# One kernel, three edits: a third home for the normalised rows of the first stage, the key-value product in four strips, and a gate by tanh in place of the sigmoid

## The reference

```python
xn = _layernorm(x, axis=-1)
x = x + _L0_attn_ref(xn, Wq, Wk, Wv) + _L0_ffn_ref(xn, Wr, br, W1, b1, W2, b2)
xn = _layernorm(x, axis=-1)
x = x + _L1_attn_ref(xn, W_qkv, W_out) + _L1_ffn_ref(xn, W_r, W_k, W_v, mu_r, mu_k)

# _L1_attn_ref, after rotation of q and k by position:
q_feat = jax.nn.elu(q * SCALE) + 1.0
k_feat = jax.nn.elu(k) + 1.0
kv = jnp.einsum('bhtd,bhtv->bhdv', k_feat, v)        # per head 16 x 16
k_sum = k_feat.sum(axis=2)
denom = jnp.maximum(jnp.einsum('bhtd,bhd->bht', q_feat, k_sum), 1e-06)
out = jnp.einsum('bhtd,bhdv->bhtv', q_feat, kv) / denom[..., None]

# _L1_ffn_ref:
r = jax.nn.sigmoid(jnp.einsum('btc,dc->btd', xr, W_r))
k = jnp.einsum('btc,dc->btd', xk, W_k)
out = r * jnp.einsum('btc,dc->btd', jnp.square(jax.nn.relu(k)), W_v)
```

## Time and profile before

| what | value |
|---|---|
| median of 3 runs | 980.91 us (980.83 to 981.66) |
| the profiled execution | 979.83 us, its span 978.2 us |
| TensorE busy | 865.8 us, 89% of the span |
| VectorE busy | 674.3 us, 69% |
| ScalarE busy | 515.4 us, 53% |
| GpSimd busy | 181.2 us, 19% |
| mean granted TensorE clock | 0.955 |

### The profile page before, as it was taken

The page is one execution under the profiler, slowest core; times in us unless marked ns, Lnnn a source line. Parts: engine busy times, 40 slices in busy tenths (PEclk is TensorE's granted clock), DMA queues, the critical chain, the costliest instruction groups (busy, mean ns, idle before and its releaser), DMA issues. The chain is left out here.

```text
span 978.2 us, 16165 instructions
## 1 busy us (share of the span) xinstructions
PE 865.8 (89%) x5619; PEld 773.9 (79%) x5619; DVE 674.3 (69%) x1287; ACT 515.4 (53%) x907; POOL 181.2 (19%) x198
## 2 busy tenths in 40 slices
PE   3898202799799999999999999999979999999998
PEld 3687101799699999899999989999878787978877
DVE  7786000454666878878787787888477979889764
ACT  3632000433555564664756465475438867678581
POOL 1004775000000000000000000000612526153202
PEclk9999555899999999999999999999989999999999
DMA  8772446000544766666567665653300203021101
GB/s 263 265 253 76 151 156 218 1 1 2 163 131 150 230 229 214 214 220 209 190 207 244 216 211 203 221 197 103 92 23 22 65 19 98 16 76 53 43 1 44
DMA packets 93871, 134.24 MB, mean 137 GB/s; under 512 B 8608, under 2 KB 78688, under 8 KB 93824
## 3 DMA queue, kind: packets, MB, share of 16 engines
q1 hardware_dynamic: 85024, 107.80, 33.6%
q0 software_dynamic: 8800, 25.83, 7.9%
HBM read 98.22 MB, written 35.39 MB: 137 GB/s over the span
## 5 line engine op out<-in xcount | busy, mean ns | idle before, releaser
L1061 PE MATMUL ps<-w2h,hh 128*128 128x256 f32 x568 | 162.8, 287 | 0.0
L1063 PE MATMUL ps<-w2h,hl 128*128 128x256 f32 x568 | 160.7, 283 | 0.0
L1062 PE MATMUL ps<-w2l,hh 128*128 128x256 f32 x568 | 160.7, 283 | 0.0
L1201 ACT ACTIVATE h<-ps,b1T 128x512 f32<-128x512 f32 (+1 forms) x160 | 90.5, 588 | 132.7 <-PE ps L1063 132.5
L1306 DVE TENSOR_TENSOR hl<-h,hh 128x512 fp32r<-128x512 f32 x124 | 85.5, 689 | 66.1 <-ACT hh L1205 65.2
L1061 PE MATMUL ps<-xTh,w1h 128*128 128x512 f32 (+1 forms) x320 | 110.7, 346 | 2.4 <-DVE xTl L1248 2.4
L1050 POOL DMA_DIRECT2D expert_out<-y x28 | 20.5, 733 | 492.3 <-DVE y L1265 492.3
L1062 PE MATMUL ps<-xTl,w1h 128*128 128x512 f32 (+1 forms) x320 | 110.6, 346 | 0.0
L1061 PEld LDWEIGHTS ps<-w2h,hh 128*128 128x128 f32 x568 | 108.7, 191 | 2.4 <-DVE hl L1306 0.2
L1062 PEld LDWEIGHTS ps<-w2l,hh 128*128 128x128 f32 x568 | 108.8, 192 | 2.1
L1063 PE MATMUL ps<-xTh,w1l 128*128 128x512 f32 (+1 forms) x320 | 109.9, 343 | 0.0
(11 more groups left out here) (306 smaller groups left out, 2262.9 us busy)
## 6 DMA issues: line engine op xcount, KB each, us to landing
raw<-in_L_ffn_W SPq DMA_DIRECT2D x30, 1024.0 KB
raw_odd<-in_L_ffn_W SPq DMA_DIRECT2D x28, 1024.0 KB, 6.8
dispatched<-shared SPq DMA_DIRECT2D x1, 9088.0 KB, 32.1
expert_out<-y POOLq DMA_DIRECT2D x11, 512.0 KB, 3.6
rows<-dispatched SPq DMA_DIRECT2D x20, 256.0 KB, 3.4
shared<-in_L_ffn_b SPq DMA_DIRECT2D x9, 512.0 KB, 8.3
xn_rows<-raw SPq DMA_DIRECT2D x4, 1024.0 KB, 5.2
rows<-xn_rows SPq DMA_DIRECT2D x32, 128.0 KB
```

Source lines behind the costliest of these rows:

```text
L1061: pe.matmul(out, ah, bh, start=start, stop=False, skip_group_check=True)
L1062: pe.matmul(out, ah, bl, start=False, stop=False, skip_group_check=True)
L1063: return pe.matmul(out, al, bh, start=False, stop=stop, skip_group_check=True)
L1201: op = act.activation(h32[:, at, cols], ps[:, slot, cols], ACT.Relu, bias=s.b1T[:, ds(e * HC + w * tile.chunks + n, 1)])
```

## The change

Three edits.

First stage. A third home for normalised rows is taken in `s.shared[:, 1]` (later the home of the attention's `prob`; the first softmax waits for the store). Sequences 0 to 3 lie in homes 0, 1, 2, 0. Sequence 1 is normalised by ScalarE (`normalized(2)`, Identity with scale rstd and bias -mean x rstd, the bias made by VectorE's `shifts(2)`); VectorE does the others. Sequence 2 no longer waits for a store, sequence 3 for that of sequence 0 alone. normalize(n) now comes ahead of statistics(n + 1), and `xl` and `al` behind the last normalize. The wait for `xn_ready` 3 on VectorE keeps the count in order.

Key values. The product is made in four strips of 32 channels: output partitions 32q to 32q + 32, 33 columns each (32 values of the strip and the column of ones), in place of 128 partitions by 129 columns. The mask reads the strip's 32 columns four times over.

Gate. tanh(x / 2) in place of sigmoid(x); the gate product is (tanh + 1) x value, and the half that is missing is put into the third weight `wT[:, 2]` as it is copied, for which that copy is split in two.

```diff
@@ first stage
-        xn = s.raw[:, :].rearrange("p (u i d) -> p u i d", u=2, i=BT)
+        xn_homes = [s.raw[:, u * BT * D:(u + 1) * BT * D].rearrange("p (i d) -> p i d", i=BT) for u in range(2)]
+        xn_homes.append(s.shared[:, 1, :].rearrange("p (i d) -> p i d", i=BT))
+        def xn(b):
+            return xn_homes[(0, 1, 2, 0)[b]]
...
             for b in range(B):
                 sp.wait_ge(xn_ready, b + 2)
-                sp.dma_start(xn_rows.rearrange("(b i p) d -> b p i d", b=B, p=P)[b], xn[:, b % 2]
-                             ).then_inc(xn_stored[b % 2], 16)
+                sp.dma_start(xn_rows.rearrange("(b i p) d -> b p i d", b=B, p=P)[b], xn(b)
+                             ).then_inc(xn_stored[(0, 1, 1, 0)[b]], 16)
...
+            def normalized(n):
+                b, tiles = UNITS[n]
+                act.wait_ge(shift_done, 1)
+                for t in tiles:
+                    op = act.activation(xn(b)[:, t % BT, :], x_tile(t), ACT.Identity,
+                                        bias=shift[:, t % BT:t % BT + 1], scale=rstd[:, t:t + 1])
+                op.then_inc(xn_ready, 1)
...
             add_bias(0)
+            normalized(2)
+            deviation(3)
             act.wait_ge(w_loaded, 48)
             act.activation(wh[:, :, :], w3[:, 2], ACT.Copy).then_inc(wh_ready, 1)
...
-            deviation(3)
             turned_out(1)
...
+                if first:
+                    act.wait_ge(xn_stored[1], 32)
                 softmax(0)
...
+            def shifts(n):
+                at = invert(n)
+                V.scalar_tensor_tensor(shift[:, :], mv[:, at, 0], -1.0, rstd[:, at], ALU.mult, ALU.mult
+                                       ).then_inc(shift_done, 1)
...
             statistics(2)
-            for n in range(2, len(UNITS)):
-                if n + 1 < len(UNITS):
-                    statistics(n + 1)
-                if n == len(UNITS) - 1:
-                    ...
-                normalize(n)
+            shifts(2)
+            statistics(3)
+            dve.wait_ge(xn_ready, 3)
+            normalize(3)
+            statistics(4)
+            normalize(4)
+            dve.wait_ge(xh_ready, 1)
+            V.tensor_tensor(xl[:, 0], ...).then_inc(xl_ready, 1)
+            dve.wait_ge(ah_ready, 1)
+            V.scalar_tensor_tensor(al[:, :, :], ...).then_inc(al_ready, 1)
@@ key values
-        v1 = sb("v1", [P, BT, DC, P + 1])
+        Q, NQ = 32, P // 32
+        v1 = sb("v1", [P, BT, DC, NQ, Q + 1])
...
                     for i in range(BT):
-                        mm = pe.matmul(ps[:, 4 + c, 0:P + 1], feat[:, i, D + c * P:D + (c + 1) * P], v1[:, i, c, :],
-                                       start=(i == 0), stop=(i == BT - 1))
+                        for q in range(NQ):
+                            of = slice(D + c * P + q * Q, D + c * P + (q + 1) * Q)
+                            mm = pe.matmul(ps[q * Q:(q + 1) * Q, 4 + c, 0:Q + 1], feat[:, i, of], v1[:, i, c, q, :],
+                                           start=(i == 0), stop=(i == BT - 1))
...
-                    V.tensor_tensor(kv[:, c, 0:P], ps[:, 4 + c, 0:P], same_head[:, :], ALU.mult)
-                    op = V.tensor_scalar(kv[:, c, P:P + HP], head_of[:, :], ps[:, 4 + c, P:P + 1], None, ALU.mult)
+                    V.tensor_tensor(kv[:, c, 0:P].rearrange("p (q f) -> p q f", f=Q),
+                                    ps[:, 4 + c, 0:Q].unsqueeze(1).to_broadcast([P, NQ, Q]),
+                                    same_head[:, :].rearrange("p (q f) -> p q f", f=Q), ALU.mult)
+                    op = V.tensor_scalar(kv[:, c, P:P + HP], head_of[:, :], ps[:, 4 + c, Q:Q + 1], None, ALU.mult)
@@ gate
-            act.activation(wT[:, :, :, :].rearrange("p n c d -> p n (c d)"), ps[:, 4:7, :], ACT.Copy
+            act.activation(wT[:, 0:2].rearrange("p n c d -> p n (c d)"), ps[:, 4:6, :], ACT.Copy)
+            act.activation(wT[:, 2].rearrange("p c d -> p (c d)"), ps[:, 6, :], ACT.Copy, scale=0.5
                            ).then_inc(weights_ready, 1)
...
-                    act.activation(gate[:, 2 * n:2 * n + 2, :], pair_of_tiles(ps[:, 4 + n, :]), ACT.Sigmoid
+                    act.activation(gate[:, 2 * n:2 * n + 2, :], pair_of_tiles(ps[:, 4 + n, :]), ACT.Tanh, scale=0.5
                                    ).then_inc(gate_ready, 1)
...
-                    V.tensor_tensor(at, pair_of_tiles(ps[:, (6 + n) % 8, :]), at, ALU.mult).then_inc(gated, 1)
+                    V.scalar_tensor_tensor(at, at, 1.0, pair_of_tiles(ps[:, (6 + n) % 8, :]), ALU.add, ALU.mult
+                                           ).then_inc(gated, 1)
```

More of the change, by code:

```diff
@@ L165, in norm_route_attend @@
         unused = sb("unused_root", [P, 1])
+        shift = sb("shift", [P, BT])
         b1r = sb("b1r", [E * s.HC, P])
@@ L188, in norm_route_attend @@
         w_loaded, small_loaded = sem("w_loaded"), sem("small_loaded")
-        const_ready, zero_ready, zero_filled = sem("const_ready"), sem("zero_ready"), sem("zero_filled")
+        const_ready, zero_filled = sem("const_ready"), sem("zero_filled")
         padded = sem("padded")
@@ L194, in norm_route_attend @@
         b1_turned, b1_ready = sem("b1_turned"), sem("b1_ready")
-        stats_done, mv_done, std_done, rstd_done, xn_ready = (sem(n) for n in (
-            "stats_done", "mv_done", "std_done", "rstd_done", "xn_ready"))
+        stats_done, mv_done, std_done, rstd_done, shift_done, xn_ready = (sem(n) for n in (
+            "stats_done", "mv_done", "std_done", "rstd_done", "shift_done", "xn_ready"))
         xn_stored = [sem(f"xn_stored{u}") for u in range(2)]
@@ L281, in _ @@
             pool.memset(brc[:, :], 0.0).then_inc(padded, 1)
-            pool.memset(zero[:, :], 0.0).then_inc(zero_ready, 1)
+            pool.memset(zero[:, :], 0.0).then_inc(padded, 1)
             pool.memset(s.ident[:, :], 0.0).then_inc(const_ready, 1)
@@ L334, in turn_tokens @@
                         mm = pe.transpose(ps[:, q, i * P:(i + 1) * P],
-                                          xn[:, b % 2, half * 4 + i, c * P:(c + 1) * P], s.ident[:, :])
+                                          xn(b)[:, half * 4 + i, c * P:(c + 1) * P], s.ident[:, :])
                     mm.then_inc(turned, 1)
@@ L611, in statistics, with invert @@
                 op.then_inc(mv_done, 1)
+            def invert(n):
+                at = slice(UNITS[n][1][0], UNITS[n][1][-1] + 1)
+                dve.wait_ge(std_done, n + 1)
+                V.reciprocal(rstd[:, at], std[:, at]).then_inc(rstd_done, 1)
+                dve.wait_ge(rstd_done, n + 1)
+                return at
+            def shifts(n):
+                at = invert(n)
+                V.scalar_tensor_tensor(shift[:, :], mv[:, at, 0], -1.0, rstd[:, at], ALU.mult, ALU.mult
+                                       ).then_inc(shift_done, 1)
             def normalize(n):
                 b, tiles = UNITS[n]
-                dve.wait_ge(std_done, n + 1)
-                at = slice(tiles[0], tiles[-1] + 1)
-                V.reciprocal(rstd[:, at], std[:, at]).then_inc(rstd_done, 1)
-                dve.wait_ge(rstd_done, n + 1)
-                if b >= 2:
-                    dve.wait_ge(turned, 4 * (b - 1))
-                    dve.wait_ge(xn_stored[b % 2], 16)
+                invert(n)
+                if b == B - 1:
+                    dve.wait_ge(turned, 4)
+                    dve.wait_ge(xn_stored[0], 16)
                 for t in tiles:
-                    op = V.tensor_scalar(xn[:, b % 2, t % BT, :], x_tile(t), mv[:, t, 0:1], rstd[:, t:t + 1],
+                    op = V.tensor_scalar(xn(b)[:, t % BT, :], x_tile(t), mv[:, t, 0:1], rstd[:, t:t + 1],
                                          ALU.subtract, ALU.mult)
@@ L1881, in body @@
                         act.activation(qk[:, n % 2, j, D:2 * D], bank[:, D:2 * D], ACT.Copy)
-                    act.activation(v1[:, 2 * n:2 * n + 2, :, 0:P],
-                                   ps[:, (6 + 3 * n) % 8, :].rearrange("p (j c f) -> p j c f", j=2, c=DC), ACT.Copy
+                    act.activation(v1[:, 2 * n:2 * n + 2].rearrange("p j c q f -> p (j c q) f")[:, :, 0:Q],
+                                   ps[:, (6 + 3 * n) % 8, :].rearrange("p (g f) -> p g f", f=Q), ACT.Copy
                                    ).then_inc(qkv_out, 1)
```

14 lines of the change are left out of this document (6 added, 8 removed).

## The result

| what | before | after |
|---|---|---|
| median, 7 runs each on one chip | 980.83 us (979.96 to 981.66) | 976.36 us (974.52 to 978.34) |
| ratio to before | | 0.9955, 95% interval 0.9943 to 0.9968 |
| the profiled execution, its span | 979.83, 978.2 us | 978.34, 976.7 us |
| mean granted TensorE clock of the profile | 0.955 | 0.945 |

The change made the kernel 4.4 us faster (3.1 to 5.6 by the interval), where the forecast said 6.6.

What follows compares the result with a forecast made beforehand. VectorE was taken to bound the first stage, VectorE close behind TensorE the last stage's loop, and TensorE alone the last sequence. Gains 4.0 + 0.4 + 2.2 = 6.6 us gave a median of 974.3, range 972.5 to 978.0.

Steps and rivals of the forecast that it cites:

- First stage, 4.0 us: Start of the kernel: fourth sequence's normalised rows ready at 30.2 instead of 34.2, moving projections and routing 4.0 us earlier.
- 2.67 for the rows: First stage, VectorE: normalising the third sequence's rows takes 2.67 us, from 20.9 to 23.6, against 28.6 before.
- Key values, 1.0 us: Last stage, TensorE: the block in four strips takes 1.0 us instead of 3.57; bounds 0.9 and 7.0.
- the router's row: Router's product in the profile: 16 passes of 256 columns on array quarters take 1.07 us, showing quarters run together.
- The wait for the squares: Last stage: strips finish before ScalarE's squares, so TensorE's next product waits; last sequence strips 951.8, squares 952.07.
- Rival (a): Key values: strips do not share their time, block stays 3.7 us, only the first stage gains: 976.9; chance 0.12.
- (c): Key values: each step of four quarters costs 0.22 us whatever its columns, block 7.0 us: 990.7, slower; chance 0.06.
- Last sequence, 2.2: Last stage, last sequence: TensorE alone sets the time; its next product starts at 952.2 instead of 954.38, 2.2 us.
- the table edit's 1.28: Last stage, ScalarE: tanh removes the 1.28 us table load before the gates in each sequence, so squares end earlier.
- Rival (d): Last stage, ScalarE: tanh brings a table load elsewhere before the squares; last sequence saves 0.9: 975.6; chance 0.04.
- First three sequences, 0.4: Last stage: of 2.1 us won, att rows and gate products leave 0.14 each, 0.4 together; bounds -0.3 and 1.5.
- rival (b): Scatter gap: the gain ahead of the routing is lost because remaining TensorE work stands behind it: 978.3; chance 0.09.

Runs made afterwards that it cites:

- first two sets: Eight kernels: the edits apart (first stage, strips, tanh, strips with tanh), then the changed kernel with fillers, GpSimd held back, VectorE reordered, all three; ratios 0.9902 and 0.9902 excluded.
- third chip: Chip of four kernels: combined follow-ups with ScalarE's normalisation moved again, 0.9902; kernel before with 14 identity turns, 0.9993; changed kernel with two strips, 0.9959; changed kernel, 0.9952.
- the kernel before with fillers: Kernel before plus 14 unread identity turns on TensorE in its hole ahead of the fourth sequence's turn; ratio 0.9993 (0.9981 to 1.0004).

## Why the prediction came out as it did

**First stage, 4.0 us: the step that was mis-sized; 2.8 measured (1.9 to 3.8).** The path was right: VectorE's and ScalarE's chain sets the fourth sequence's rows, and routing, scatters and experts follow the projections. Two terms were not.
- The sum took each duration from a profile at clock 1.00 and set it against the median of all runs; it gave the clock no term. Three of four profiles with the old first stage and its hole have half clock at this turn, so has each of the five with the new order and its hole (2.3 to 2.9 us). So the projections move from 41.0 to 37.9 and not from 39.57 to 35.6. On these means the turn itself starts 3.7 us earlier (34.5 to 30.8), and 0.6 more are lost between it and the projections (6.5 us before, 7.1 after). A sign of it could be had: that profiled run lay 1.1 us under the median, and the forecast carried this over as a constant.
- "2.67 for the rows" of the third sequence took no account of GpSimd. Moved ahead by 5 us, they fall on its 128x512 subtraction. Two of the eight passes of after, and that subtraction:

```profile
20.82 1.70 DVE L649 TENSOR_SCALAR shared<-x_acc,mv,rstd 128x256 f32<-128x256 f32 x2
```

```profile
21.08 1.28 POOL L310 TENSOR_TENSOR folded<-shared,folded 128x512 fp32r<-128x512 f32 x1 [17.51 <-ACT folded L545]
```

These two passes end at 22.52, 0.16 us behind the subtraction's end at 22.36. The second of them takes 1.37 us, where the others take 0.40 each: it started 0.07 us behind the subtraction and was held up until this was done. That is the 0.96 us by which 3.63 exceeds the 2.67 of the eight passes without GpSimd beside them. The Trainium skill states this in "SBUF — State Buffer", Who interferes with whom: a VectorE operation in a 2-port mode and a GpSimd operation exclude each other for a whole instruction, and the one that comes second is blocked, not slowed. The trace agrees on the block; in which mode the passes ran it does not show.

**Key values, 1.0 us: 1.30 measured,** in the bounds and by the router's row, as argued: the strips share their time. The wait for the squares that was forecast behind them is there in the first sequence alone; in the last the strips end later than forecast and the squares before them, so the 2.2 us came out right with another of the two as the last to end, 0.2 us apart. Rival (a) needed a block of 3.5 us or more and (c) one of 4.6, so both are out. The Trainium skill, "TensorEngine Tiling (Array Packing)", Instruction Overhead, gives the estimate of 3.2 us for passes that do not share; the trace does not agree with it for strips side by side, with 128 passes in 1.30 us.

**Last sequence, 2.2: 2.15.** The strips alone, 0.9 forecast by way of the table edit's 1.28: 0.88. Rival (d) is out, no table load stands before the gates.

**First three sequences, 0.4: 174.29 for 174.49, 0.2.** TensorE was stopped at att and gate products, at the places named, for att by 1.05 us in the third (1.5 forecast).

**The gap, rival (b).** From the projections to the experts' first product it is 217.6 us in the first-stage-only kernel (254.90 - 37.32) and 217.4 in the profile of before (256.96 - 39.57). Over the ten profiles of the first two sets and of the result it lies between 216.9 and 218.1, with 217.9 after the change, so a loss of the whole gain, as (b) has it, is out, and one of half a microsecond can't be told from noise. On the third chip, where TensorE works through the scatters, the changed kernel takes 143.1 us for this stretch and the kernel before with fillers 141.9, and of 2.0 us won at the projections 0.8 are left at the experts (181.54 to 180.71). From 78 to 92 us the clock is 0.76 in the one and 0.88 in the other.

**What stays open.** By rows strips and tanh bring 2.35 us after the change and 2.5 in the kernel with both alone, by the times of the kernel with both only 1.2 (0.3 to 2.1). The three-way sum fits: 2.8 + 1.2 = 4.0 and 4.4 measured for all. Stretches of half clock of differing length also stand near 80 us, at the experts' start and before the last stage, in most profiles: 256 to 262 us has 0.72 before and 0.50 after. From the experts' first product to the last stage's, where the kernels differ in the weight copy alone, the ten profiles take 486.4 to 488.2 us. I take the missing 1.2 us for such chance; that spread is large enough for it, but no run shows it.

## What to carry to other kernels

Before a forecast is set against a median, compare the clock of the profiled run with the other runs' and price the stretches that stand at full clock behind a hole. Where a short serial chain of TensorE follows a hole of two or three microseconds, try filling it: here that shortened the chain in the rows, by an amount the times could not confirm. When work is moved on VectorE, look at GpSimd's row for the time it moves to. A wait removed from a tight loop is to be followed to the next engine by a wait table of the new kernel before it is counted: here 4 us of waits on att gave 1.2, then 2.7.

## What the runs showed of the hardware

The gap of the scatters is not a property of the kernel. In all ten profiles of the result and the first two sets TensorE works 2.6 to 5.9 of the 20 us from 100 to 120 us; on the chip of the third set it works all 20.00 in each of four profiles. The same scatters go on beside it; those of the changed kernel end there at 164.09 us (after, first profile: 164.59). The changed kernel there:

```profile
100.00:120.00 20.00, 20.00 (x140) 18.00 (x140) 10.31 (x14) 8.89 (x13) 15.24 (x16) 1.00 0.49 159
...
180.71 0.50 PE L1087 MATMUL ps<-xTh,w1h 128*128 128x512 f32 x1 [2.37 <-DVE xTl L1274]
```

The experts start at 180.71 in place of 256.98, and the median of before is 899.83 us, 81 less. In the first profile of after ScalarE and VectorE each stand once for a long time with no semaphore to wait for ("issue"), and TensorE waits behind them; in the 60 us from 100 on no packet comes in on the queue q8 of instructions, and on the third set's chip three do. The waits of the first and the queue of the second:

```profile
ACT vh L571 <- issue: 51.0, 1, 51.0
DVE vl L694 <- issue: 32.6, 1, 32.6
```

```profile
q8 instruction: 3, 0.05, 0.5%
```

The engines may have run out of instructions behind the indirect transfers; that is a guess from these rows, and no run tests it. What makes one chip differ from another was not tried. The ratio of the change was the same on both, 0.9955 and 0.9952.
